# A second cross-attention whose weighing matmul streams 128 value columns instead of 32

## The reference, cut to what matters

```python
q = _fq_sym(q * scale, axis=-1)          # (16 heads, 64 rows, 16)
k = _fq_sym(k, axis=-1)                  # (16, 6272, 16)
v = _fq_sym(v, axis=2)                   # one step for each value column
attn = jnp.einsum('bhqd,bhkd->bhqk', q, k)
attn = jax.nn.softmax(attn, axis=-1)
attn = _fq_unsigned(attn, axis=-1)       # integers 0..255 times a step
out = jnp.einsum('bhqk,bhkd->bhqd', attn, v)
out = out.reshape(B, N, C) @ Wp + bp
```

## Time and profile before

| | |
|---|---|
| median of 3 runs | 1170.39 us (1168.82 to 1174.01) |
| profiled execution | 1170.96 us, its span 1169.1 us |
| mean granted clock of PE over the span | 0.964 |
| PE busy | 1069.6 us (91%) |
| DVE busy | 755.1 us (65%) |
| ACT busy | 396.1 us (34%) |

### The profile page before, as it was taken

The page is one execution under the profiler, slowest core; times in us unless marked ns, Lnnn a source line. Parts: engine busy times, 40 slices in busy tenths (PEclk is TensorE's granted clock), DMA queues, the critical chain, the costliest instruction groups (busy, mean ns, idle before and its releaser), DMA issues.

```text
span 1169.1 us, 22182 instructions
## 1 busy us (share of the span) xinstructions
PE 1069.6 (91%) x8373; PEld 708.2 (61%) x8390; DVE 755.1 (65%) x1914; ACT 396.1 (34%) x724; POOL 153.2 (13%) x143
## 2 busy tenths in 40 slices
PE   6999999997777778999899999999999998988888
PEld 4767666754344545346577777777777776743454
DVE  4767676777687744336867676767676767754344
ACT  1333333343176641133333333333333332311203
POOL 0000000001000010001423232323232323000000
PEclk9999999999898779988999999999999999899999
DMA  7100001022100039830000000000000000132530
GB/s 262 36 25 31 24 30 28 12 74 82 58 1 1 1 150 323 298 138 1 1 1 1 1 1 0 0 0 0 0 0 0 0 1 1 72 127 80 212 131 3
DMA packets 17947, 64.61 MB, mean 55 GB/s; under 512 B 1376, under 2 KB 8288, under 8 KB 14432
## 3 DMA queue, kind: packets, MB, share of 16 engines
q1 hardware_dynamic: 17456, 63.08, 15.0%
q10 hardware_dynamic: 432, 0.72, 0.2%
HBM read 63.73 MB, written 0.07 MB: 55 GB/s over the span
## 4 chain that ended last, share of the span: by engine, by line
PE 75%; DVE 9%; issue 8%; POOL 3%; ACT 3%; DMA 1%; SPq 0%; DVEq 0%; POOLq 0%
PE ps L2179 15%; PE ps L2140 11%; PE ps L1462 7%; PE ps L2169 7%; PE ps L1452 4%; PE ps L1473 4%; PE ps L1846 3%; PE ps L1496 2%; POOL x_sum L2651 2%; PE ps L1508 2%; PE ps L2100 2%; ACT wide L2009 1%; PE ps L1861 1%; PE ps L2725 1%; PE ps L502 1%
## 5 line engine op out<-in xcount | busy, mean ns | idle before, releaser
L2179 PE MATMUL ps<-vals,S 128*128 128x257 f32 x784 | 188.1, 383 | 0.7 <-ACT S L2584 0.7
L2140 PE MATMUL ps<-keysT,row_biases_sb 128*128 128x512 f32 (+1 forms) x416 | 185.9, 573 | 0.0
L2651 POOL TENSOR_TENSOR x_sum<-x_max,consts 128x4 f32<-128x4 f32 (+1 forms) x104 | 133.9, 1288 | 380.8 <-DVE x_max L2372 380.8
L2384 DVE SCALAR_TENSOR_TENSOR S<-ps,x_sum,keysT 128x128 f32<-128x128 f32 x392 | 111.0, 345 | 78.2 <-PE ps L2179 67.0
L2179 PEld LDWEIGHTS ps<-vals,S 128*128 128x128 f32 x784 | 143.0, 192 | 18.9 <-issue 1.0
L2584 ACT ACTIVATE S<-S 128x512 f32<-128x512 f32 (+1 forms) x104 | 62.7, 606 | 220.3 <-DVE S L2419 219.8
L2169 PE MATMUL ps<-x_q,x_keys 128*128 128x128 f32 x784 | 112.9, 286 | 0.0
L2140 PEld LDWEIGHTS ps<-keysT,row_biases_sb 128*128 128x128 f32 x416 | 77.2, 192 | 55.9 <-issue 51.6
L2169 PEld LDWEIGHTS ps<-x_q,x_keys 128*128 128x128 f32 x784 | 95.4, 191 | 0.0
L1462 PE MATMUL ps<-ring,S 128*128 128x512 f32 x196 | 92.7, 595 | 0.5 <-DVE ps L1603 0.5
L2572 ACT COPY x_keys<-ps 128x512 f32<-128x512 f32 (+1 forms) x104 | 57.1, 549 | 64.0 <-PE ps L2169 33.2
(11 more groups left out here) (455 smaller groups left out, 1563.2 us busy)
## 6 DMA issues: line engine op xcount, KB each, us to landing
ring<-weights SPq DMA_DIRECT2D x24, 1024.0 KB, 4.9
keysT<-ctxT SPq DMA_DIRECT2D x1, 6272.0 KB, 18.8
vals<-ctxN SPq DMA_DIRECT2D x1, 6272.0 KB, 25.1
S<-ctxT SPq DMA_DIRECT2D x12, 512.0 KB, 3.9
keysT<-weights SPq DMA_DIRECT2D x6, 864.0 KB, 8.6
ring<-weights SPq DMA_DIRECT2D x6, 768.0 KB, 6.4
ring<-weights SPq DMA_DIRECT2D x2, 864.0 KB, 5.4
row_biases_sb<-row_biases SPq DMA_DIRECT2D x1, 1416.0 KB, 12.1
```

Of the source, the lines that this page charges most:

```text
L2140: ins = pe.matmul(ps[:, c % 3, 0:width(c)], x2_wk[:, k, :], ctxT[:, k, span(c)], start=k == 0, stop=k == KT - 1)
L2179: ins = pe.matmul(bank(6, D + 1), S[:, a:a + TILE], ctx_and_ones[:, SUB * c + s, :], start=c == 0 and s == 0, stop=c == NC - 1 and s == su ...
L2384: ins = dve.scalar_tensor_tensor(S[:, a:a + TILE], ps[:, 3 + c % 2, 128 * s:128 * s + 128], x2_inv[:, c % 2, s:s + 1], x2_tile_const, ALU. ...
L2651: pool.tensor_tensor(x2_inv[:, c % 2, 0:n], x2_var[:, c % 2, 0:n], C("neg_half").broadcast_to([128, n]), ALU.pow)\
```

## The change

`weigh` streams 128 value columns instead of 32: those of the four pairs of heads to which its own pair belongs. The product is 128 rows x 128 columns in the same bank; `finish` reads from it the 32 columns of its own pair. The other 96 columns (these probabilities with other heads' values) are not read. Nothing else is changed: same counts of instructions, same order, same waits.

```diff
@@ x1_tensor, weigh(j, e)
-                    ins = pe.matmul(ps[:, 6 + j % 2, 0:32], x1_probsT[n % 2][:, s, :], vals_int[:, x1_tile(GROUP * e + s), 32 * j:32 * j + 32],
+                    ins = pe.matmul(ps[:, 6 + j % 2, 0:128], x1_probsT[n % 2][:, s, :], vals_int[:, x1_tile(GROUP * e + s), 128 * (j // 4):128 * (j // 4) + 128],
                                     start=e == 0 and s == 0, stop=e == PROB_GROUPS - 1 and s == GROUP - 1)
@@ x1_vector, finish(j)
-                dve.tensor_scalar(x1_out[:, 32 * j:32 * j + 32], ps[:, 6 + j % 2, 0:32], x1_total, None, ALU.mult).then_inc(sem("x1_tile_done"), 1)
+                dve.tensor_scalar(x1_out[:, 32 * j:32 * j + 32], ps[:, 6 + j % 2, 32 * (j % 4):32 * (j % 4) + 32], x1_total, None, ALU.mult).then_inc(sem("x1_tile_done"), 1)
```

## The result

| | before | changed |
|---|---|---|
| median of 15 runs | 1168.82 us (1164.02 to 1175.42) | 1162.72 us (1161.29 to 1169.07) |
| profiled execution | 1170.96 us, span 1169.1 | 1161.96 us, span 1160.0 |
| mean granted clock over the span | 0.964 | 0.980 |

The ratio of the two is 0.9951, with a 95% interval of 0.9933 to 0.9970: the change makes the kernel 6 us faster, though PE streams four times the columns at line 1870. The kernel before, at 1170.39 us in the three runs that the prediction had, is at 1168.82 over fifteen.

What follows compares the result with a forecast made beforehand. The prediction took a PE-DVE ping-pong over score banks, plus falls to half clock, to bound the stage. Terms -5.73 + 0.3 + 0 - 0.4 = -5.8 us gave 1164.6 us against the 1170.39 median; range 1161.0 to 1171.5.

Steps and rivals of the forecast that it cites:

- (a): Wider weighs: each group of seven takes 0.22 us more PE time at full clock, 0.53 at half.
- (b): Pair loop at full clock: added columns fit PE's waits for DVE, leaving 0.61 us; pairs stay 12.69 us, cost 0.
- (c): Stage opening at half clock: one weigh before a set of scores without room, up to +0.53, taken as +0.3 us.
- (d): Pair loop: extra PE work in the waits removes all three falls to half clock, -5.73 us.
- Three of six windows: Pair loop, cut between successive scores(j, 3): three windows took 12.69 us at full clock, the others 13.88, 13.99 and 15.93.
- stretch "without a fall": Pair loop: PE busy 2.71 us of 4.00 without a clock fall following, against 2.12, 2.22 and 2.55 ahead of falls.
- (e): Last pair, paced by ACT: -0.2 us if the clock stays full, +1.9 if half; taken as 0.
- the case at full clock: Last pair with the clock staying full: last turn gains 0.38 us, last weigh goes from 0.37 to 0.55, -0.2.
- The third rival: Pair loop keeps full clock but the last pair stays at half: -3.5 us, 1166.9 us; chance 0.23.
- (f): Projection and filler behind the stage: partly faster clock, -0.4 us; ends 0 and -2.2 if full clock lasts through both.
- The first rival: Clock does not respond, falls stay in the loop and columns cost half-clock time: +3.0 us, 1173.4 us; chance 0.13.
- the two classes: Whole kernel's outcome: faster by more than 0.5%, chance 0.43, or within 0.5%, chance 0.50.

Runs made afterwards that it cites:

- the covered kernel: Changed kernel plus unread matmuls, 70 of 128 columns around the first pair's scores and three of 512 before the projection: 1160.9 and 1159.9 us.

## Why the prediction was right

**The forecast** was 1164.6 us, -0.50%; measured 1162.7 and 0.9951. The mechanism is the one named. That the sum came out right is partly luck: it took 2.2 us too much for the loop (5.73 against 3.5 on average) and had nothing for the 2.8 us that the stretches outside the change gave in these profiles.

(a) The columns: 0.33 to 0.55 us for a group at full clock, as the transposes had said; at half clock 0.40 to 0.95 in the opening, where 0.93 was expected. Right.

(b) Hidden: 12.69 us for a pair with 0.61 us of room at all three places, as worked out. Right; the runs with 256 columns and with 10 rows show both ends of it, a cover that is used up at full clock and one that is used up at half.

(c) The opening: +0.3 was expected, and the profile has 18.19 against 18.72 us. The two can't be compared as they are, since the clock falls one set of scores later in the changed kernel's. Profiles with the fall at the same place can: the kernel before and the one with a narrow last pair (whose opening is the changed kernel's), then the second of the kernel before and the changed kernel:

```profile
307.41:326.13 18.72, 12.17 (x108) 6.35 (x108) 13.90 (x21) 7.72 (x13) 0.00 (x0) 0.73 0.00 1
```

```profile
307.89:326.99 19.10, 13.07 (x109) 7.27 (x108) 13.90 (x21) 7.72 (x13) 0.00 (x0) 0.73 0.00 1
```

```profile
306.80:324.78 17.98, 11.54 (x108) 6.25 (x107) 13.95 (x21) 7.72 (x13) 0.00 (x0) 0.81 0.00 1
```

```profile
306.50:324.69 18.19, 12.15 (x109) 7.06 (x108) 13.96 (x21) 7.72 (x13) 0.00 (x0) 0.81 0.00 1
```

The columns cost 0.38 us with the early fall and 0.21 with the late one (0.29 and 0.40 in two more profiles, 18.27 and 18.38). The term is right; in this execution a later fall hid it.

(d) The clock in the loop: all falls gone, in both profiles and in six variants. Right as a mechanism, but the size, -5.73, is that of one execution; the kernel before loses 3.5 us on average over three. The step that failed is the reading of a price that changes from run to run from a single profile. "Three of six windows" looked like a property of the kernel and was one draw.

The comparison with a stretch "without a fall" (2.71 us of 4.00) doesn't carry what was rested on it. That stretch lies at another place within its pair than the three others. Taken at their places, the same pair, which had no fall and was followed by another without one, gives their numbers to 0.01 us:

```profile
334.96:338.96 4.00, 2.12 (x37) 1.30 (x38) 3.64 (x7) 3.95 (x7) 0.00 (x0) 1.00 0.00 0
334.73:338.73 4.00, 2.21 (x38) 1.39 (x34) 3.64 (x7) 4.00 (x7) 0.00 (x0) 1.00 0.00 0
334.40:338.40 4.00, 2.54 (x47) 1.72 (x44) 3.64 (x5) 3.75 (x6) 0.00 (x0) 1.00 0.00 0
```

The same work led to a fall in one pair and to none in another, so how busy PE was in such a stretch doesn't tell which pair falls. That a little more work is enough for the loop was a guess from these rows; the run with 64 columns is what shows it. What picks the pair stays open.

(e) The last pair: 16.10 against 16.28 us, the -0.2 of the case at full clock. The sum took 0, between the two cases. The third rival, which had the last pair at half, was wrong: in the last pair too the wide weighs held the clock. The Trainium skill, "TensorE: Matmul & The Clock Gate", Part 4 (PE-mode transpose), says that transposes don't count as busy for the clock; here the measurement differs. With five transposes behind each group the clock was at 1.00 through all six pairs, as with matmuls (76.14 us in both). So the kind of the work is not enough to explain the half level in the last pair of the kernel before. Its amount matters: in the kernels whose loop stays at full, the last pair's mean clock is 0.82 and 0.83 with 32 columns, 0.95 with 64 and 1.00 with 128. That transposes count for less than matmuls isn't excluded.

(f) What comes after: 6.37 us against 7.31, -0.9, where -0.4 was taken; its far end of -2.2 is what the covered kernel and the one with 256 columns reach (5.07 and 5.06, so -2.2).

What the sum lacked: 1.3 us from stage 6 on. The prediction's last sentence named this, the falls of the clock in the other stages, as what could shift it. The profiles show 688.3 to 691.7 us there for the same instructions (693.8 in the run with 10 rows), and the value goes with the time at which stage 6 starts (above). So a shorter stage 3 can be worth more or less than its own microseconds, by more than 3 us between starts less than 1 us apart (472.67 and 473.39); why the start matters stays open.

The chances: the measured ratio lies on the bound of 0.5% between the two classes to which 0.43 and 0.50 were given. The first rival (the clock doesn't respond) is refuted by the changed kernel and by six of the seven variants; something like it came true in the one where the extra work has 10 rows.

## What to carry to other kernels

When PE waits in a loop for another engine, look at its granted clock window by window before counting its work: equal windows with unequal lengths, and a clock under 1.00 in the long ones, are a hint that idle time is costing PE its speed. Work put into such a wait is free as long as it is shorter than the wait, and over all 128 rows it may pay for itself; here 64 columns did as well as 128, while extra work over 10 rows made the kernel 1% slower. Take such a price from several profiles: one execution lost 5.7 us to it and another 1.3.

## What the runs showed of the hardware that was not expected

- Extra matmuls over 10 rows cost PE as much time as over 128 (two of 336 columns 0.74 and 0.72 us at half clock) and did not bring the clock back: PE busy 18.03 of 18.03 us at 0.50.
- bf16 transposes of 128 rows count for the clock: 76.14 us for six pairs with 640 extra columns as transposes, and the same with 672 as matmuls.
- The stages from 6 on took 688.3 to 688.5 us when stage 6 started at 470.4 to 472.7 us, and 691.6 to 691.7 when it started at 473.4 to 476.0, with the same instructions and mean clocks of 0.98 and 0.97.
